# A four-layer block on one core: each bf16 part of q and k stored once, and repeated by the loads of both attentions

## What is computed

```python
x = x + attn_a(layernorm(x))   # wave attention
x = x + ffn(layernorm(x))
x = x + attn_b(layernorm(x))   # distance attention
x = x + ffn(layernorm(x))
```

```python
# attn_a
sim = q @ k.T / sqrt(8) / temp
scores = sum(alpha[h, f] * sin(2 * pi * sim / FREQS[f] + phi[h, f]) for f in range(5))
w = sigmoid(scores); w = w / (w.sum(-1) + 1e-10)
# attn_b
scores = q @ k.T / sqrt(8) + q . pos_emb[i - j] + k . pos_emb[i - j]
w = softmax(scores)
```

## Time and profile before

| | us |
|---|---|
| median of 3 runs | 4173.84 |
| lowest and highest of them | 4168.84, 4179.46 |
| the profiled execution | 4163.56 |
| its span, from first to last instruction | 4161.80 |
| mean granted TensorE clock | 0.921 of full speed |

### The profile page before, as it was taken

How to read it: one execution, slowest core, us unless ns; L and a number is a source line. 1 busy time by engine, 2 the same in 40 slices (tenths; PEclk the granted TensorE clock), 3 DMA queues, 4 the chain that set the end, 5 groups by cost and what they waited for, 6 DMA issues and landing times. The chain is left out here.

```text
span 4161.8 us, 71345 instructions
## 1 busy us (share of the span) xinstructions
PE 3403.4 (82%) x27092; PEld 2090.7 (50%) x27092; DVE 3438.3 (83%) x4264; ACT 2880.8 (69%) x2433; POOL 1126.6 (27%) x983
## 2 busy tenths in 40 slices
PE   3799999999999999999938933688988888897990
PEld 2233333333333333333336932587887887887790
DVE  7899999999999999999847634678788787787662
ACT  3799999999999999999804313466665666664530
POOL 2111221121121112112101541535334335321235
PEclk8899999999999999999967966799999999998995
DMA  4100000000000000000032226411202102102122
GB/s 132 30 6 13 13 13 6 13 13 10 9 13 13 6 13 13 13 6 13 5 106 72 68 52 138 81 25 32 45 18 47 31 17 47 30 18 64 34 65 66
DMA packets 145098, 146.44 MB, mean 35 GB/s; under 512 B 62673, under 2 KB 123697, under 8 KB 140113
## 3 DMA queue, kind: packets, MB, share of 16 engines
q1 hardware_dynamic: 136144, 125.04, 12.3%
q0 software_dynamic: 8704, 17.84, 1.8%
HBM read 90.73 MB, written 52.10 MB: 34 GB/s over the span
## 5 line engine op out<-in xcount | busy, mean ns | idle before, releaser
L704 PE MATMUL psA<-wave,diag 128*128 128x512 f32 x3072 | 1433.9, 618 | 138.2 <-DVE score L860 86.7
L772 ACT ACTIVATE wave<-wave 128x2048 f32<-128x2048 int32 x640 | 1180.8, 1904 | 3.3 <-DVE wave L847 2.2
L704 PEld LDWEIGHTS psA<-wave,diag 128*128 128x128 f32 x3072 | 579.8, 195 | 893.2 <-issue 693.6
L641 POOL TENSOR_TENSOR diag<-ident,par 128x128 f32<-128x128 f32 x384 | 298.1, 803 | 1431.2 <-PE psA L704 1431.2
L822 DVE TENSOR_SCALAR wave<-s,par 128x2048 int32<-128x2048 int32 x480 | 610.6, 1272 | 0.0
L847 DVE TENSOR_SCALAR wave<-wave 128x2048 int32<-128x2048 int32 x512 | 608.0, 1211 | 0.0
L1735 POOL COPY kb<-ks 48x1024 bf16<-48x1024 bf16 x160 | 330.7, 2067 | 590.3 <-PE psR L1795 421.9
L1876 ACT COPY r<-psR 128x1024 f32<-128x1024 f32 x320 | 310.7, 1025 | 163.0 <-PE psR L1795 163.0
L737 ACT ACTIVATE s<-psS,par 128x1024 int32<-128x1024 f32 x256 | 282.8, 1105 | 128.8 <-PE psS L667 128.8
L1885 ACT ACTIVATE W<-psR 128x1024 f32<-128x1024 f32 x256 | 253.4, 1025 | 167.7 <-PE psR L1820 164.8
L860 DVE SCALAR_TENSOR_TENSOR score<-wave,par,psA 128x1024 f32<-128x1024 f32 x256 | 317.2, 1268 | 35.0 <-PE psA L704 35.0
(11 more groups left out here) (259 smaller groups left out, 4444.0 us busy)
## 6 DMA issues: line engine op xcount, KB each, us to landing
ks<-kb_parts SPq DMA_DIRECT2D x56, 384.0 KB, 6.2
qs<-qb_parts SPq DMA_DIRECT2D x32, 384.0 KB, 6.2
ys<-f_ys SPq DMA_DIRECT2D x36, 256.0 KB, 2.5
wave_out<-og SPq DMA_DIRECT2D x33, 256.0 KB, 2.1
o<-wave_out SPq DMA_DIRECT2D x8, 1024.0 KB, 5.2
qp<-qa_parts SPq DMA_DIRECT2D x32, 192.0 KB, 3.5
kp<-ka_parts SPq DMA_DIRECT2D x32, 192.0 KB, 3.9
f_wu<-in_w_up SPq DMA_DIRECT2D x2, 2048.0 KB, 10.3
```

Of the source, the lines that this page charges most:

```text
L641: ins = pool.tensor_tensor(diag[:, h % 2, f, :], ident[:], par[:, u, 1, h * NF + f:h * NF + f + 1] .to_broadcast((P, P)), ALU.mult)
L704: mm = pe.matmul(psA[:, kt, :], diag[:, h % 2, f, :], wave[:, h % 2, f, kt * L:(kt + 1) * L], start=(f == 0), stop=(f == PE_F - 1), skip_g ...
L772: act.activation(wave[:, h % 2, f, :], angle[:, h % 2, f, :], ACT.Sin, scale=float(TWO_PI / 2.0 ** 32)).then_inc(sine, 1)
```

## The change

The projections store each part once: 3 row blocks of 8 rows for each side, 24 rows in DRAM instead of 48. The orders of the six blocks become `hhhmml` for q and `hmlhmh` for k, which pair the same six products. The table `COPIES` says how the 24 rows become 48: entries are (first row in the tile, first row in DRAM, number of rows, how many times). In `wave_attention` each repetition is a transfer of its own. In `distance_attention` an entry is one transfer, whose source repeats its rows with a step of zero in front. The semaphore counts follow.

```diff
-LEFT = "hhmhlm"
-RIGHT = "hmhlhm"
+LEFT = "hhhmml"
+RIGHT = "hmlhmh"
+COPIES = {"q": ((0, 0, HD, 3), (3 * HD, HD, HD, 2), (5 * HD, 2 * HD, HD, 1)),
+          "k": ((0, 0, 3 * HD, 1), (3 * HD, 0, 2 * HD, 1), (5 * HD, 0, HD, 1))}
...
-            n: nc.dram_tensor(n, (B * H, NR, L), BF16, kind="Internal").ap()
+            n: nc.dram_tensor(n, (B * H, 3 * HD, L), BF16, kind="Internal").ap()
...
-            dram[n] = nc.dram_tensor(n, (NR, QT, B * H, P), BF16, kind="Internal").ap()
+            dram[n] = nc.dram_tensor(n, (3 * HD, QT, B * H, P), BF16, kind="Internal").ap()
...
-                for s, (_, dst, order) in enumerate(sides):
-                    for r, w in enumerate(order):
-                        if r == 0:
-                            sp.wait_ge(high, b * NS + s + 1)
-                        if w == "l":
-                            sp.wait_ge(low, b * NS + s + 1)
-                        if w == "m":
-                            sp.wait_ge(mid, b * NS + s + 1)
+                for s, (_, dst) in enumerate(sides):
+                    for r, (w, ready) in enumerate((("h", high), ("m", mid), ("l", low))):
+                        sp.wait_ge(ready, b * NS + s + 1)
...
+        QK_LOAD = 16 * sum(times for src in "qk" for _, _, _, times in COPIES[src])
+
         def load(sp, g, u):
-            for dst, src in ((qp, "qa_parts"), (kp, "ka_parts")):
-                sp.dma_start(dst[:, u, :, :], dram[src][bass.ds(g * HG, HG), :, :]
-                             .rearrange("h r n -> r h n")).then_inc(qk_loaded[u], 16)
+            for dst, src in ((qp, "q"), (kp, "k")):
+                for at, first, n, times in COPIES[src]:
+                    rows = dram[src + "a_parts"][bass.ds(g * HG, HG), first:first + n, :].rearrange("h r n -> r h n")
+                    for i in range(times):
+                        sp.dma_start(dst[at + i * n:at + (i + 1) * n, u, :, :], rows).then_inc(qk_loaded[u], 16)
...
                 for at in (0, ODD):
-                    sp.dma_start(dst[at:at + NR, :, :],
-                                 dram[src][:, t, g * BH:(g + 1) * BH, :]).then_inc(landed, 16)
+                    for row, first, n, times in COPIES[src]:
+                        rows = dram[src + "b_parts"][first:first + n, t, g * BH:(g + 1) * BH, :]
+                        sp.dma_start(dst[at + row:at + row + n * times, :, :],
+                                     rows.rearrange("(a r) h n -> a r (h n)", a=1)
+                                     .to_broadcast((times, n, BH * P))).then_inc(landed, 16)
```

More of the change, by code:

```diff
@@ L165, in project_block @@
     wave = layer == "a"
-    sides = [("q", "qa_parts", LEFT), ("k", "ka_parts", RIGHT)] if wave else \
-            [("q", "qb_parts", LEFT), ("k", "kb_parts", RIGHT)]
+    sides = [("q", "qa_parts"), ("k", "ka_parts")] if wave else [("q", "qb_parts"), ("k", "kb_parts")]
     NS = len(sides)
@@ L238, in project_block @@
         nload = 6 + (3 if wave else 0)
-        each = 16 * len(LEFT)
+        each = 16 * 3
         @block.sync
@@ L694, in pair @@
                             if nh == 0:
-                                pe.wait_ge(qk_loaded[nu], (gg + 1 + u) * 32)
+                                pe.wait_ge(qk_loaded[nu], (gg + 1 + u) * QK_LOAD)
                             make_scores(n + 2, nu, nh, 0)
@@ L714, in pair @@
                             values(g, 1 - u, (h, h + 1))
-            pe.wait_ge(qk_loaded[0], 32)
+            pe.wait_ge(qk_loaded[0], QK_LOAD)
             for h in range(2):
@@ L1528, in distance_attention @@
     KS = QT - 1
+    TILE_LOAD = 2 * 16 * len(COPIES["q"])
     KB = 2
@@ L1686, in load_q @@
                     sp.wait_ge(filled, fill["c", (q - 2) * QT + QT - 1, 3] + 1)
-                load(qs[:, q % 2, :, :], "qb_parts", q, q % QT, qs_loaded[q % 2])
+                load(qs[:, q % 2, :, :], "q", q, q % QT, qs_loaded[q % 2])
             def load_k(u):
@@ L1691, in load_k @@
                     sp.wait_ge(filled, fill["c", k_loads[u], 3] + 1)
-                load(ks[:, ks_of(u), :, :], "kb_parts", u // QT, tile_of(u), ks_loaded[ks_of(u)])
+                load(ks[:, ks_of(u), :, :], "k", u // QT, tile_of(u), ks_loaded[ks_of(u)])
             def load_v(g):
@@ L1722, in _ @@
                     load_v((u + 1) // (QT * QT))
-            for landed, n in ((t_loaded, 32), (v_loaded, 16 * B), (qs_loaded[0], 16 * NQ), (qs_loaded[1], 16 * NQ)):
+            for landed, n in ((t_loaded, 32), (v_loaded, 16 * B), (qs_loaded[0], TILE_LOAD * NQ // 2), (qs_loaded[1], TILE_LOAD * NQ // 2)):
                 sp.wait_ge(landed, n)
             for at in range(KS):
-                sp.wait_ge(ks_loaded[at], 32 * sum(1 for u in k_loads if ks_of(u) == at))
+                sp.wait_ge(ks_loaded[at], TILE_LOAD * sum(1 for u in k_loads if ks_of(u) == at))
         @block.gpsimd
@@ L1740, in spread_q @@
             def spread_q(q):
-                pool.wait_ge(qs_loaded[q % 2], 32 * (q // 2 + 1))
+                pool.wait_ge(qs_loaded[q % 2], TILE_LOAD * (q // 2 + 1))
                 for half in range(2):
@@ L1747, in spread_k @@
             def spread_k(u):
-                pool.wait_ge(ks_loaded[ks_of(u)], 32 * k_landed(u))
+                pool.wait_ge(ks_loaded[ks_of(u)], TILE_LOAD * k_landed(u))
                 if k_spreads[u] is not None:
@@ L1803, in content @@
                     pe.wait_ge(act_took, by_act["r1", u, CH - 1])
-                    pe.wait_ge(ks_loaded[ks_of(u)], 32 * k_landed(u))
+                    pe.wait_ge(ks_loaded[ks_of(u)], TILE_LOAD * k_landed(u))
                 slot = free_slot(fill["c", u, k]).rearrange("p a (h n) -> p (a h) n", n=P)
```

## The result

| | before | changed |
|---|---|---|
| median of the runs, us | 4171.83 (6 runs, 4166.75 to 4179.46) | 4134.8 (6 runs, 4129.72 to 4138.64) |
| ratio to before, with its interval | | 0.9911 [0.99, 0.9922] |
| profiled execution, us (span) | 4163.56 (4161.8) | 4131.55 (4129.8) |
| written to HBM, MB | 52.10 | 39.52 |

The change saves 37 us by the medians and 32.0 by the two profiled executions; the forecast was 44.8. The same two kernels on another occasion gave 4135.9 and 4169.06, ratio 0.9925 [0.9909, 0.994].

The account below looks back on a forecast made before the run. SP's issue queue was taken to bound both projection stages. -21.2 + 1.0 - 31.5 + 6.9 = -44.8 us, from 4173.8 to 4129 us; range 4115 to 4150.

Parts of the forecast that it names:

- Layer a: Projections of layer a: 48 of 96 issues go, VectorE then sets the pace; minus 21.2 us, between 19 and 22.
- Head of wave attention: Start of wave attention: the first group's q and k need nine transfers instead of two; plus 1.0 us, bounds 0 and 2.4.
- Layer b: Projections of layer b: seven issues a batch, the TensorE and ScalarE loop nearly equal at 4.85 us; minus 31.5 us.
- Rival 4: Projections: TensorE's clock stays at its lower level, layer b gains 13 us less, total 4142 us; chance 0.05.
- Head of distance attention: First q tile of distance attention: few rings, 34 rows on the first, 13.9 us instead of 7.0; plus 6.9 us.
- rival 2: Distance attention's q loads: a ring moves a row in 0.6 to 0.83 us, total 4137 to 4155 us; chance 0.2.
- Body: Distance attention behind its head: later q and k tiles still arrive in time; 0 us.
- All rings: Distance attention: q transfers spread over all rings after all; minus 51.7 us, total 4122 us; chance 0.15.
- Slow rings: Distance attention's q loads: a ring takes 0.6 to 0.83 us a row, total 4137 to 4155 us; chance 0.2.
- Held-up k tiles: Distance attention: a q tile's few rings delay each k tile behind it; plus 81 us, total 4255; chance 0.05.
- Low clock: Projections: TensorE's clock stays at its lower level, gain 13 us less, total 4142 us; chance 0.05.
- Signs: Wrong if the first q tile takes 7 or over 20 us, GpSimd waits for `qs` later, or a batch exceeds 6.

Follow-up runs that it names:

- only_a: Against the before kernel, only layer a is changed; layer b stores and loads 48 rows as before: 4151.03 us (5 runs), ratio 0.9963.
- separate: Against the changed kernel, each repetition of q rows in distance attention is its own transfer of 8 rows: 4135.58 us in one execution.
- alone: Against the changed kernel, SP waits for distance attention's first q tile to land before issuing further loads: 4116.21 us in one execution, later 4130.75 (6 runs).
- alike: Against the changed kernel, k's parts are stored low, middle, high, so both sides load as contiguous runs: 4124.45 us (4 runs), later 4119.81 (5 runs).
- one_ring: Against `alike`, each half q tile goes in six transfers of 23, 1, 13, 3, 7 and 1 rows: 4147.13 us in one execution.

## Why the prediction was right, and where its terms were off

**What bounds the kernel: right for layer a, likely for layer b.** With half of SP's issues gone, the stages shrank to the pace of VectorE (5.59 us a batch, as forecast) and of the loop of TensorE and ScalarE (4.85, as forecast). `only_a` shows the half of layer a by itself; the DMA engines were about 70% busy there, so it was SP's issues that bounded it. In layer b the prediction left out a rival: before the change the DMA engines were busy for 0.90 to 0.96 of most 5 us stretches, so the stores themselves may have bounded that stage together with SP's issues. The change takes away both, and no run separates them. For it to be SP speaks that a store landed 2.5 to 2.8 us after its issue (medians), before and after, with no growing backlog. At 4.85 us a batch the DMA engines are 0.93 to 0.95 busy again, so by an estimate from these shares little more than 0.3 us a batch was left to win (4.85 x 0.06).

**Layer a, -21.2 forecast, -16.7 measured.** Wave attention starts at 96.59 us, not 92.1. Four pieces make up the 4.3 us by which VectorE's last result is late: v of batch 0 is taken at 43.52 us where the profile of before has 40.96, +2.6; batches 1 to 6 +0.2; batch 7 comes 5.19 us behind batch 6 where I took 4.75, +0.4; the last result is 5.7 us behind batch 7's v, not 4.6, +1.1. GpSimd adds 0.3. For the last piece the profile of before already had 6.0 us (90.31 to 96.31); the 4.6 was too small as read. The first piece is an anchor read from one profile. In the ten profiles of the seven kernels here with the shorter stores, batch 0's v came at 41.9 to 43.8 us and the stage ended between 94.8 and 97.5, so a single reading has two to three us of play, and the forecast's "between 19 and 22" was too narrow. All ten have that v later than the one profile of before; whether the change does that stays open.

**Head of wave attention, +1.0 forecast, +1.7 measured** (4.85 to 6.59 us). The issues took 2.04 us for q and 1.33 for k, 3.37 in all against 3.2 forecast. No later group was held up: wave attention took 1971.7 us against 1971.6.

**Layer b, -31.5 forecast, -29.5 measured.** 1.7 us of the missing 2 is the last batch at 6.52 us instead of 4.85, with TensorE at its lower clock for part of it. That is no accident of one profile: in all nine profiles of kernels with the shorter stores in layer b the last batch took 6.25 to 6.52 us. Rival 4, the clock that stays low, came true for one batch of eight.

**Head of distance attention, +6.9 forecast, +18.1 measured: the mis-sized term.** The step that failed is "I take 0.35 [...] and add a tenth for the other loads beside them". The prediction had also said that it would be wrong if the first q tile took over 20 us, and it took 25.1. Its ring counts were right, by 26 small packets and by 1120 packets in `separate`. The Trainium skill's rule (DMA: Bandwidth & Descriptors, section "Why a DMA increments its semaphore by 16 and not by 1") agrees with every count here. Its row rate was right for a ring alone: 13.4 us for a lone tile, 13.95 in `alone`, 13.9 forecast. Wrong was the allowance for company, a tenth (1.1 us) where `alone` shows 11 us. In the changed kernel the head is busy with everything at once (DMA view over 2574 to 2594 us, then that of before over 2612 to 2632):

```profile
DMA  4215799697999979799686777886978476834466
...
DMA packets 655, 2.92 MB, mean 146 GB/s; under 512 B 215, under 2 KB 299, under 8 KB 341
```

```profile
DMA packets 641, 3.29 MB, mean 165 GB/s; under 512 B 143, under 2 KB 239, under 8 KB 287
```

Some 12 of the 16 DMA engines are busy, yet together they move 146 GB/s, 12 GB/s each; alone, one ring moved 27. Before had the same company and 165 GB/s, but its q tile needed 6 rows of the busiest ring, and now 34. A slow ring costs with the rows on it, and the first ones cost most: by the last table of the experiments the start of the copy moved by 0.86 us a row from 6 rows to 12, by 0.59 from 12 to 34, and by 0.37 from 34 to 56, which is near the 0.30 of a ring alone. These kernels differ in the number of transfers too, so the three figures are estimates. My argument for the fast end, that "three rings ask for far less in total", looked at the tile and not at what is issued 4 us behind it. The rows had it: the key tile moved at 161 GB/s over 16 rings, 0.83 us a row. The head's 25.1 us are (25.1 - 2.0) / 34 = 0.68 us a row, an average over a busy and a quiet part, and that is rival 2's size. Rival 2's total of 4137 to 4155 us lies just above the median of 4134.8. The loads of the head together moved 146 GB/s with few rings, 147 in `alike` and 165 before, though the expert weights moved 416 over the same rings; that suggests a limit shared by these loads, and which one it is was not tried.

**Body, 0 forecast.** GpSimd's wait for `ks` rose from 160.9 to 177.4 us in 15 times and TensorE's wait for its k stayed at 7.1 to 7.2 us in 3, so the cover held, as worked out. The stage itself was 6.9 us shorter, and `one_ring` had it back at 1180.3. Two profiles of the same kernel agree better than that, to 0.7 us for the changed kernel and `alone` and to 2.9 for `alike`, so it may not be chance. What makes the body differ between kernels stays open.

**Rivals.** All rings: excluded by 26 packets. Slow rings: true at the head, not for a lone tile. Held-up k tiles: not at 34 rows nor at 56. Low clock: one batch.

**Signs.** Two of the signs of being wrong came: the first q tile took over 20 us, and one projection batch, the last of layer b, over 6. The expected gaps of SP's queue in layer a are there, but 15.3 us of them wait for ScalarE's middle parts and 3.8 for VectorE's low parts.

**The total.** -32.0 us by the profiles, -37.0 by the medians, against -44.8. The two projection terms were 6.5 us too large together and those of the heads 12.4 us too small (0.7, and 11.7 by the head stage's 18.6), which makes -25.9; the rest of the program gave the other 6.2, most of it in the body of distance attention. So the total came nearer than its terms: part of the error is hidden by those 6.2, which I had not forecast, and that is luck. The forecast of 4129 us is 5.8 below the median; had before's median been 4173.8 again and not 4171.83, the same saving would leave it 7.8 below.

## What to carry to other kernels

When a queue's own issue time bounds a stage, count its issues and then ask what pace is next, the busy share of the DMA engines among them; the rows that show it are already in the profile of before. When a repeated source or a short slowest dimension puts a transfer on few rings, price it twice: alone, and with what is issued right behind it, since at the busy head a row took about twice as long. If the order of rows is yours to choose, choose one in which the copies are contiguous runs: that was 16.1 us less here for the same bytes and as many stores.

## What the runs showed that I had not expected

- A transfer with a repeated source takes SP longer to issue: 3.89 us for six against 2.12 us for six plain ones of the same sizes, 0.63 and 0.31 us each by the medians over the program. In `alike` q too takes 2.15.
- The second q tile's six issues took 12.98 us at the head (17.65 us for twelve k issues in `one_ring`): SP was held at the issue itself. In `alike` and `separate`, with the same bytes under way, the second q tile was issued in 2.15 and 4.01 us, so this comes with rows piled on few rings and not with bytes.
- One ring alone moved 8 KB rows at 27 GB/s, while at the busy head about 12 rings moved 12 GB/s each.
- 13 rows run on 13 rings, 24 on 12: the number of rings is not monotone in the number of rows, and 23 rows use one.
